# Three changes to a four-layer image kernel on one core: where group statistics are taken, which output sums are added first, and the instruction order of a spline attention

## The chip, the cores and the metric

The kernel runs on one core of one Trainium2 chip. The time is the device time of one launch in microseconds (us); lower is better. Everything is float32.

A core has TensorE (PE, matrix products; its weight loads are shown as PEld), VectorE (DVE), ScalarE (ACT) and GpSimd (POOL), each with an instruction queue of its own that is worked off in order; SyncE (SP) issues the transfers. The engines wait for one another by semaphores. SBUF is the on-chip memory with 128 partitions, PSUM the memory that PE writes its products to.

## The reference

`x` is (2, 256, 56, 56). Four layers are applied in turn, each to the group-normalised `x`, and each is added to `x`. `_gn` normalises over groups of 8 channels and all pixels of an image.

```python
x = x + _L0_conv_ref(_gn(x), ...)   # 7x7 neighbourhood attention, 8 heads, no softmax
x = x + _L1_conv_ref(_gn(x), ...)   # 4x4 depthwise blur
x = x + _L2_conv_ref(_gn(x), ...)   # channel gate, then softmax attention over all 3136 pixels
x = x + _L3_conv_ref(_gn(x), ...)   # attention whose scores pass a spline, 4 heads of 32
```

The last layer takes nearly all of the time:

```python
sim = jnp.einsum('bhnd,bhdm->bhnm', q, k) / math.sqrt(dh)      # 2 images, 4 heads, 3136 x 3136
xs = jnp.clip(sim, -6, 6)
kan = base_w * silu(xs) + jnp.einsum('...k,k->...', b_splines(xs), coef)   # cubic spline
attn = softmax(kan, axis=-1)
out = jnp.einsum('bhnm,bhmd->bhnd', attn, v)
```

Every score needs a clip, the silu, a cubic spline with knots 2.4 apart, and the exponential.

## The kernel before, in words

`x` stays in SBUF as `X`, 128 partitions by 4 units (image times channel half) by 3136 pixels. The layers follow one another: `opening`, `attention0` for image 0 and image 1, `group_norm_stats` "1", `blur1`, `group_norm_stats` "2", `attention2`, `group_norm_stats` "3", `attention3`. Every function is one or more blocks, and at a block's end all engines meet, so what one engine does there counts unless another of the same block ends later.

**Group statistics.** `group_norm_stats` (L373) issues 28 `bn_stats` on DVE, one for each unit and each chunk of 448 pixels (L400), aggregates them with four `bn_aggr` (L403), and a short chain over PE and ACT makes `m.rstd` and `m.nbias`. For "2" the 28 `bn_stats` were already issued inside `blur1` (L970).

**Output of layer 0.** `project_out0` (L850) goes through eight spans of columns for two channel halves f, 16 jobs in all. PE makes a sum in one of eight PSUM banks (L866), DVE adds it to `X` (L879). The five spans of 500 columns (50 by 10 inner pixels) come first, then three spans for the borders of the image: 314, 294 and 48 columns; the last is four small pieces of 9 or 12 elements for each half.

**Projections of layers 0 and 2.** In `project_queries0` (L452) DVE normalises one unit (L461) and is then idle while PE and ACT make the queries. In `project2` (L1063) DVE makes the gated input (L1087) and then adds a bias to seven chunks (L1091), while POOL adds the gated input to `X` of the same image (L1080) and ACT copies the other two projections.

**Spline attention.** `kan_attention3` (L1483) handles 196 blocks: 2 images by 2 pairs of heads by 49 tiles of 64 queries. The 128 partitions hold 64 queries of each of two heads. The 3136 keys of a block are four quarters g of 784 (two PSUM banks of 392, index j). For one quarter:

- PE `scores(g)` makes the raw scores into `scp` (L1617).
- DVE `clip(g, 0)` and `clip(g, 1)` write `x` (L1696), 392 elements each.
- ACT `tanh` writes S back into `scp` (L1779); `magnitude` makes `a = |x|` (L1787); `beyond` makes `v1 = relu(a - 1.2)` and `v2 = relu(a - 3.6)` (L1795); `squared` their squares `s1`, `s2` (L1804).
- POOL `line` and `square` make `inner`, the polynomial part (L1580, L1587); `cube(g, 0)` and `cube(g, 1)` turn the squares into cubes (L1594).
- PE `right_side(g)` makes `up`, the part of the spline that holds for positive x only, from the cubes and two diagonal matrices (L1630).
- DVE `gate(g)` writes `up` where x > 0 into `prob` (L1689), `add_tanh` starts `fp` (called a_kan in the trace, L1707), `times_x` multiplies (L1714), `left(g, 0)` and `left(g, 1)` add the cubes (L1725), `add_right` sums into `prob` and finds the maximum (L1735).
- `row_max` (L1750) and `negated_max` (L1755) make the softmax shift once a block; ACT `exponent` (L1831) applies it; PE `turn` transposes `prob` in seven chunks (L1642), ACT `copies` moves each to SBUF (L1812), PE `weigh` multiplies it with V (L1652). `invert` (L1746), `place` (L1820), `fold_heads` (L1670), `keep_o` (L1826), `project_out` (L1662) and `add_output` (L1742) finish a block.

The order of each engine's queue is written out by hand: a list of (stage, lag), walked by `pipeline_pairs` (L1330), where lag is how many blocks behind the newest one the stage works. One walk is four **slots** g = 0..3, one per quarter. On DVE slot g clips quarter g of the newest block and finishes the quarter three slots back (called g3), and its last instruction is the gate of the quarter two back:

```python
order += [(add_tanh(g3), l3)] + between[0] + [(times_x(g3), l3)] + between[1] + [(left(g3, 0), l3), (clip(g, 0), 0), (left(g3, 1), l3),
          (clip(g, 1), 0), (add_right(g3), l3), (gate(g2), l2)]
```

`between` holds the small ones: invert in slot 1 and row_max in slot 3 behind add_tanh, add_output in slot 2 and negated_max in slot 3 behind times_x. Three handshakes tie the slots together. `scores` of a slot waits for that slot's `add_tanh`, because S and the scores share PSUM; the slot's first clip waits for `scores`. `tanh` on ACT waits for the slot's last clip, and the next slot's `add_tanh` waits for `tanh`. `gate` waits for `right_side`, which waits for the cubes. `invert` (slot 1) waits for `weigh(6)`, which PE issues in slot 0.

Of the kernel before, what the change touches and what calls it, by code (L numbers as in the profile page):

```python
# [7 lines left out]
F32 = mybir.dt.float32  # L8
ALU = mybir.AluOpType
# [4 lines left out]
B = 2  # L14
# [122 lines left out]
def conv_preact_kernel(nc, x, qkv_w, qkv_b, proj_w, proj_b, rel_bias, fir, cfc, theta_w, theta_b,  # L137
                       phi_w, phi_b, g_w, g_b, out_w, out_b, wq3, wk3, wv3, wo3, base_w, spline_w,
                       spline_scaler, mask_dram, spline_m, out):
    with ExitStack() as ctx:  # L140
        def sb(name, shape):
            return ctx.enter_context(nc.sbuf_tensor(name, shape, F32))
# [21 lines left out]

        m.onehot = sb("onehot", [KEYS, ONEHOT_W])
        bias_dram = nc.dram_tensor("bias_rows_dram", (BIAS_ROWS, BIAS_ROW), F32, kind="Internal").ap()

        with ExitStack() as early:
# [5 lines left out]
            stats2 = early.enter_context(nc.sbuf_tensor("blur_stats", [P, UNITS, CHUNKS, 6], F32))  # L174
            blur1(nc, m, stats2)
            group_norm_stats(nc, m, "2", stats2)
        attention2(nc, m)
        group_norm_stats(nc, m, "3")
# [194 lines left out]
def group_norm_stats(nc, m, tag, counted=None):  # L373

    with ExitStack() as st:
        sem = st.enter_context(signals(nc, tag))
        sb = lambda name, shape: st.enter_context(nc.sbuf_tensor(name + tag, shape, F32))
        stats = counted if counted is not None else sb("stats", [P, UNITS, CHUNKS, 6])
# [9 lines left out]
        with nc.Block() as block:  # L388
            @block.vector
            def _(dve):  # L390
# [6 lines left out]
                if counted is None:  # L397
                    for u in range(UNITS):
                        for k in range(CHUNKS):
                            link(dve.bn_stats(stats[:, u, k, :], m.X[:, u, CHUNK * k:CHUNK * (k + 1)]))  # L400
                    dve.wait_ge(chain, done[0])
# [50 lines left out]
def project_queries0(nc, m, b, xn, Q, O, qb, scale):  # L452
    with ExitStack() as st:
        sem = st.enter_context(signals(nc, f"p0_{b}"))
        qp = [st.enter_context(nc.psum_tensor(f"qp{i}_{b}", [P, 8, IMG], F32)) for i in range(4)]
        normed, cleared, q_made, q_placed, qb_ready = (sem(n) for n in ("xn_ready", "cleared", "q_made", "q_placed", "qb_ready"))
        with nc.Block() as block:
            @block.vector
            def _(dve):
# [3 lines left out]
                dve.wait_ge(qb_ready, 1)  # L463

# [385 lines left out]
def project_out0(nc, m, b, O):  # L850

    with ExitStack() as st:
        sem = st.enter_context(signals(nc, f"p0_{b}"))
        yp = [st.enter_context(nc.psum_tensor(f"yp{i}_{b}", [P, 512], F32)) for i in range(8)]
        y_made, y_added = sem("y_made"), sem("y_added")
        slots = EXTRA + DX_STEP
        spans = [(500 * k, 500) for k in range(5)] + [(slots, 314), (PAIR0 + 6, 294), (CORNER0, 48)]
        with nc.Block() as block:
# [11 lines left out]
            def _(dve):  # L870
                for n in range(2 * len(spans)):
# [12 lines left out]
                    if k < 5:  # L884
                        add(img[:, 3 + 10 * k:13 + 10 * k, 3:53], grid(0, 10, GRID, GRID))
                    elif k == 5:
                        add(img[:, 0:3, 3:53], grid(0, 3, DX_STEP, GRID))
                        add(img[:, 53:56, 3:53], grid(3 * DX_STEP + BOTTOM_SHIFT, 3, DX_STEP, GRID))
                    elif k == 6:
# [7 lines left out]
                    last[0].then_inc(y_added, 1)  # L897
                dve.wait_ge(y_added, 2 * len(spans))
# [164 lines left out]
def project2(nc, m, b, theta, phi, gT, gate_scale, gate_bias):  # L1063

    with ExitStack() as st:
# [3 lines left out]
        gated, made, kept_a, kept_v, with_s = (sem(n) for n in ("gated", "made", "kept_a", "kept_v", "with_s"))  # L1069
# [3 lines left out]
        with nc.Block() as block:  # L1073
# [10 lines left out]
            def _(dve):  # L1084
# [3 lines left out]
                for k in range(CHUNKS):  # L1088
# [3 lines left out]
                                      m.gbias[low:P, :].unsqueeze(1).to_broadcast([P - low, tiles, P]), ALU.add).then_inc(kept_v, 1)  # L1092
                dve.wait_ge(kept_v, CHUNKS)
# [389 lines left out]
def kan_attention3(nc, m, k3, out):  # L1483
# [3 lines left out]
    with ExitStack() as st:  # L1487
# [10 lines left out]
        v1 = [sb(f"v1{g}", [P, QUART]) for g in range(2)]  # L1498
# [373 lines left out]
```

## Time and profile before

| what | value |
|---|---|
| median of 3 runs | 7107.38 us (7102.32 to 7118.62) |
| the profiled execution | 7109.38 us, span 7107.3 us |
| busy: PE, DVE, ACT, POOL | 6218.9, 6060.1, 5703.7, 5398.8 us |
| mean granted clock of TensorE | 0.969 of full speed |
| moved by DMA | 79.83 MB, mean 11 GB/s |

The busy shares in tenths, in 40 slices of the span (178 us each), show the layers: nine or ten slices for layers 0 to 2, then thirty of one unchanging pattern.

```profile
PE   6777899996888888888888888888888888888888
DVE  5444444444999999999999999999999999999998
ACT  5372332333999999999999999999999999999998
POOL 4351000003999999999999999999999999999997
```

In the trace an instruction's record runs from the start of its execution to the acknowledged write, and the record of the next may begin before that end. So what an instruction takes of its engine is read from one start to the next, not from its duration; this is called its **step** below.

### The profile page before, as it was taken

What the parts mean: (1) busy time and instruction counts of PE and PEld (TensorE: products, weight loads), DVE (VectorE), ACT (ScalarE), POOL (GpSimd) and SP (SyncE); (2) the same over time, 40 slices, a digit from 0 to 9 for tenths busy, and PEclk for the clock granted to TensorE, in tenths of its full rate; (3) what the DMA queues carried; (4) which work ended last, traced back from release to release, by engine and by line L of the source; (5) the groups of instructions that cost most, each with busy time, mean ns of one, the idle gap of its engine ahead of it and who ended that gap; (6) DMA issues with size and microseconds to landing.
All of it is one profiled execution on the core that took longest, in us unless ns stands there. A gap on an engine that the chain in (4) does not pass through costs nothing. (4 is left out here: it accounts for less than half of the span.)

```text
span 7107.3 us, 136255 instructions
## 1 busy us (share of the span) xinstructions
PE 6218.9 (88%) x38014; PEld 4169.0 (59%) x38014; DVE 6060.1 (85%) x9428; ACT 5703.7 (80%) x8984; POOL 5398.8 (76%) x3379
## 2 busy tenths in 40 slices
PE   6777899996888888888888888888888888888888
PEld 4545676763555555555555555555555555555555
DVE  5444444444999999999999999999999999999998
ACT  5372332333999999999999999999999999999998
POOL 4351000003999999999999999999999999999997
PEclk8786999997999999999999999999999999999999
DMA  3221000002000000000000000100000000000000
GB/s 98 67 69 44 1 0 0 0 0 65 11 1 1 1 1 1 1 11 1 1 1 1 1 1 2 29 1 1 1 1 1 1 2 1 4 4 4 4 4 6
DMA packets 110735, 79.83 MB, mean 11 GB/s; under 512 B 68490, under 2 KB 108290, under 8 KB 109826
## 3 DMA queue, kind: packets, MB, share of 16 engines
q1 hardware_dynamic: 107306, 77.71, 3.8%
q8 instruction: 77, 1.26, 0.1%
q10 hardware_dynamic: 3288, 0.33, 0.0%
q14 instruction: 64, 0.52, 0.0%
HBM read 48.70 MB, written 22.86 MB: 10 GB/s over the span
## 5 line engine op out<-in xcount | busy, mean ns | idle before, releaser
L1594 POOL TENSOR_TENSOR a_s<-a_s,a_v 128x784 f32<-128x784 f32 x1568 | 2910.7, 1856 | 310.0 <-ACT a_s L1804 298.1
L1630 PE MATMUL a_right_sides<-a_s,diag_d 128*128 128x392 f32 x6272 | 2288.9, 508 | 14.7 <-POOL a_s L1594 1.0
L1630 PEld LDWEIGHTS a_right_sides<-a_s,diag_d 128*128 128x128 f32 x6272 | 1134.3, 191 | 1064.7 <-POOL a_s L1594 345.3
L1725 DVE SCALAR_TENSOR_TENSOR a_kan<-a_s,spline_c,a_kan 128x784 f32<-128x784 f32 x1568 | 1622.2, 1035 | 51.4 <-DVE a_kan L1714 0.9
L1587 POOL TENSOR_TENSOR a_inner<-a_inner,a_x 128x784 f32<-128x784 f32 x784 | 1458.9, 1861 | 0.0
L1804 ACT ACTIVATE a_s<-a_v 128x784 f32<-128x784 f32 x1568 | 1335.2, 852 | 4.6
L1795 ACT ACTIVATE a_v<-a_a 128x784 f32<-128x784 f32 x1568 | 1335.1, 852 | 0.3
L1652 PEld LDWEIGHTS a_weighed<-a_V,a_probT 128*128 128x128 f32 x9800 | 1232.4, 192 | 162.2
L1652 PE MATMUL a_weighed<-a_V,a_probT 128*128 128x65 f32 x9800 | 1223.5, 269 | 0.0
L1642 PE MATMUL a_turned<-ident,a_prob 128*128 128x128 f32 x4900 | 794.0, 280 | 325.8 <-ACT a_probT L1812 323.7
L1617 PE MATMUL a_scores<-a_K,a_q 32*64 32x392 f32 x6272 | 703.8, 515 | 273.0 <-DVE a_kan L1707 241.8
L1696 DVE TENSOR_SCALAR a_x<-a_scores 128x392 f32<-128x392 f32 x1568 | 876.1, 559 | 19.2 <-PE a_scores L1617 19.2
L1779 ACT ACTIVATE a_scores<-a_x 128x784 f32<-128x784 f32 x784 | 649.0, 828 | 260.3 <-DVE a_x L1696 248.1
L1642 PEld LDWEIGHTS a_turned<-ident,a_prob 128*128 128x128 f32 x4900 | 560.2, 147 | 465.4 <-ACT a_probT L1812 350.4
L1714 DVE SCALAR_TENSOR_TENSOR a_kan<-a_kan,linear,a_x 128x784 f32<-128x784 f32 x784 | 817.8, 1043 | 14.1
L1707 DVE SCALAR_TENSOR_TENSOR a_kan<-a_scores,half_base,a_inner 128x784 f32<-128x784 f32 x784 | 811.7, 1035 | 0.0
L1580 POOL TENSOR_SCALAR a_inner<-a_x,spline_c 128x784 f32<-128x784 f32 x784 | 782.9, 999 | 0.0
L1812 ACT COPY a_probT<-a_turned 128x512 f32<-128x512 f32 (+2 forms) x1372 | 724.5, 528 | 56.9 <-PE a_turned L1642 39.9
L1689 DVE SCALAR_TENSOR_TENSOR a_prob<-a_x,a_right_sides 128x784 f32<-128x784 f32 x784 | 757.0, 966 | 13.5 <-PE a_right_sides L1630 13.5
L1735 DVE CUSTOM_DVE_ANT_0 a_prob<-a_kan,a_prob 128x784 f32<-128x784 f32 x784 | 756.8, 965 | 0.6 <-DVE a_kan L1725 0.6
L1831 ACT ACTIVATE a_prob<-a_prob,a_nmax 128x784 f32<-128x784 f32 x784 | 735.3, 938 | 0.0
L1787 ACT ACTIVATE a_a<-a_x 128x784 f32<-128x784 f32 x784 | 662.6, 845 | 19.3 <-DVE a_x L1696 17.0
(198 smaller groups left out, 5293.8 us busy)
## 6 DMA issues: line engine op xcount, KB each, us to landing
rows<-bias_rows_dram SPq DMA_DIRECT2D x112, 91.0 KB
ve<-v_dram SPq DMA_DIRECT2D x98, 104.0 KB
X<-in_x_dram SPq DMA_DIRECT2D x4, 1568.0 KB, 13.8
xn<-kt SPq DMA_DIRECT2D x56, 112.0 KB, 2.2
v_dram<-vt SPq DMA_DIRECT2D x56, 112.0 KB, 2.0
a_q<-q_dram SPq DMA_DIRECT2D x392, 16.0 KB, 2.0
mask<-in_window_mask_dram SPq DMA_DIRECT2D x56, 98.0 KB, 1.9
a_V<-v_dram SPq DMA_DIRECT2D x4, 812.5 KB, 8.6
```

What stands on the lines that cost most here:

```text
L1580: eng.tensor_scalar(inner[g % 2][:, :], x[g][:, :], c[:, 0:1], c[:, 1:2], ALU.mult, ALU.add).then_inc(line_made, 1)
L1587: eng.tensor_tensor(z, z, x[g][:, :], ALU.mult).then_inc(inner_made, 1)
L1594: eng.tensor_tensor(s, s, v, ALU.mult).then_inc(cubed, 1)
L1630: mm = eng.matmul(up[:, j, 0:SUB], steps[i][:, :], cubes[g][:, SUB * j:SUB * (j + 1)], start=(i == 0), stop=(i == 1))
L1642: mm = eng.transpose(tp[:, j, :], prob[r][:, at:at + P], m.ident[:, :])
L1652: mm = eng.matmul(op[:, :], probT[(r + ch) % 2][:, j, :], V[p % 2][:, k, :], start=(k == 0), stop=(k == KEY_TILES3 - 1))
L1696: eng.tensor_scalar(x[g][:, SUB * j:SUB * (j + 1)], scp[:, j, 0:SUB], 6.0, -6.0, ALU.min, ALU.max).then_inc(clipped, 1)
L1707: eng.scalar_tensor_tensor(F, S, half_base[:, :], banked(inner[g % 2][:, :]), ALU.mult, ALU.add).then_inc(with_tanh, 1)
L1714: eng.scalar_tensor_tensor(F, F, linear[:, :], banked(x[g][:, :]), ALU.add, ALU.mult).then_inc(based, 1)
L1725: eng.scalar_tensor_tensor(F, banked((s1, s2)[j][g][:, :]), c[:, 3 + j:4 + j], F, ALU.mult, ALU.add).then_inc(left_added, 1)
L1795: eng.activation((v1, v2)[j][g % 2][:, :], a[:, :], ACT.Relu, bias=(-KNOT_IN, -KNOT_OUT)[j]).then_inc(v_ready, 1)
L1804: eng.activation((s1, s2)[j][g][:, :], (v1, v2)[j][g % 2][:, :], ACT.Square).then_inc(s_ready, 1)
```

## The change

It does three things.

1. **Statistics inside projections.** One buffer `m.stats` holds all units' statistics. For "1", image 0's 14 `bn_stats` are issued in `project_queries0` of image 1, and image 1's 14 in its `project_out0`, as chunks of rows become final. For "3", image 0's 14 are issued in `project2` of image 1, two behind each chunk's bias add; image 1's 14 stay in `group_norm_stats`.
2. **Border sums first.** In `project_out0` the three border spans come ahead of the five inner ones.
3. **Spline attention.** On DVE the gate is cut into two halves of 392, now in the slot of its own quarter, one ahead of and one behind `add_tanh`; the second clip is cut into two pieces of 196; the clips stand between the instructions of the chain; the small ones stand behind the first gate half. `row_max` is dropped: `add_right` stores the negated values and their minimum, and `exponent` applies scale -1. On ACT the two squares become one instruction of 1568 elements, behind the late copy. On POOL the two cubes become one of 1568, behind line and square. On PE four of the seven `turn` go right behind a `scores`, `turn(6)` with one more block of lag.

```diff
-def group_norm_stats(nc, m, tag, counted=None):
+def group_norm_stats(nc, m, tag, units=()):
...
+                for u in units:
+                    for k in range(CHUNKS):
+                        link(dve.bn_stats(stats[:, u, k, :], m.X[:, u, CHUNK * k:CHUNK * (k + 1)]))
@@ project_queries0, vector
                 dve.wait_ge(qb_ready, 1)
+                if b:
+                    for v in range(HALVES * (b - 1), HALVES * b):
+                        for k in range(CHUNKS):
+                            dve.bn_stats(m.stats[:, v, k, :], m.X[:, v, CHUNK * k:CHUNK * (k + 1)]).then_inc(counted, 1)
+                    dve.wait_ge(counted, HALVES * CHUNKS)
@@ project_out0
-        spans = [(500 * k, 500) for k in range(5)] + [(slots, 314), (PAIR0 + 6, 294), (CORNER0, 48)]
+        spans = [(slots, 314), (PAIR0 + 6, 294), (CORNER0, 48)] + [(500 * k, 500) for k in range(5)]
...
+                    if b == B - 1 and f == 1 and k >= 3:
+                        dve.wait_ge(y_added, n + 1)
+                        whole = range((10 * k - 27) // 8, (10 * k - 17) // 8 if k < 7 else CHUNKS)
+                        for v in range(HALVES):
+                            for c in whole:
+                                dve.bn_stats(m.stats[:, HALVES * b + v, c, :], ...).then_inc(counted, 1)
@@ project2, vector, in the loop over chunks k
+                    if b:
+                        for v in range(HALVES * (b - 1), HALVES * b):
+                            dve.bn_stats(m.stats[:, v, k, :], m.X[:, v, CHUNK * k:CHUNK * (k + 1)]).then_inc(counted, 1)
@@ kan_attention3, gpsimd
-                    order += [(line(g2), l2), (cube(g2, 1), l2), (square(g2), l2), (cube(g1, 0), l1)]
+                    order += [(line(g2), l2), (square(g2), l2), (cubes(g1), l1)]
@@ kan_attention3, tensor
-                pipeline_pairs(pe, [(scores(0), 0), (right_side(2), 1), (weigh(5), 3), (weigh(6), 3), (turn(0), 2),
-                                      (scores(1), 0), (project_out, 4), (right_side(3), 1), (turn(1), 2), (weigh(0), 2), (turn(2), 2),
-                                      (fold_heads, 3), (scores(2), 0), (right_side(0), 0), (weigh(1), 2), (turn(3), 2), (weigh(2), 2), (turn(4), 2),
-                                      (scores(3), 0), (right_side(1), 0), (weigh(3), 2), (turn(5), 2), (weigh(4), 2), (turn(6), 2)])
+                pipeline_pairs(pe, [(scores(0), 0), (turn(6), 3), (right_side(2), 1), (weigh(5), 3), (weigh(6), 3), (turn(0), 2),
+                                      (scores(1), 0), (project_out, 4), (right_side(3), 1), (turn(1), 2), (weigh(0), 2),
+                                      (fold_heads, 3), (scores(2), 0), (turn(2), 2), (right_side(0), 0), (weigh(1), 2), (turn(3), 2), (weigh(2), 2),
+                                      (scores(3), 0), (turn(4), 2), (right_side(1), 0), (weigh(3), 2), (turn(5), 2), (weigh(4), 2)])
@@ kan_attention3, vector
-                        eng.scalar_tensor_tensor(banked(part(r, g)), banked(x[g][:, :]), 0.0, U, ALU.is_gt, ALU.mult).then_inc(right_gated, 1)
+                        eng.scalar_tensor_tensor(part(r, g)[:, at], x[g][:, at], 0.0, up[:, j, 0:SUB], ALU.is_gt, ALU.mult).then_inc(right_gated, 1)
...
+                        first, end = ((0, SUB), (SUB, SUB + SUB // 2), (SUB + SUB // 2, 2 * SUB))[j]
...
-                        eng.tensor_tensor_reduce(out=f, in0=F, in1=f, scale=1.0, scalar=-3.0e38, op0=ALU.add, op1=ALU.max,
+                        eng.tensor_tensor_reduce(out=f, in0=F, in1=f, scale=-1.0, scalar=3.0e38, op0=ALU.add, op1=ALU.min,
...
+                    eng.tensor_reduce(nmax[r][:, :], gmin[r][:, :], AX.X, ALU.min).then_inc(max_ready, 1)
...
+                    g3, l3 = (g - 3) % 4, int(g < 3)
+                    small = {1: [(invert, 3)], 2: [(add_output, 4)], 3: [(negated_max, 1)]}.get(g, [])
+                    order += [(gate(g3, 0), l3)] + small + [(add_tanh(g3), l3), (gate(g3, 1), l3), (times_x(g3), l3), (clip(g, 0), 0), (left(g3, 0), l3),
+                              (clip(g, 1), 0), (left(g3, 1), l3), (clip(g, 2), 0), (add_right(g3), l3)]
@@ kan_attention3, scalar
-                    order += [(tanh((g - 2) % 4), int(g < 2))] + [(keep_o, 3)] * (g == 2) + [(magnitude(g), 0), early, (beyond(g, 0), 0), e, (beyond(g, 1), 0),
-                              (squared(g, 0), 0), late, (squared(g, 1), 0)]
+                    order += [(tanh((g - 2) % 4), int(g < 2))] + [(keep_o, 3)] * (g == 2) + [(magnitude(g), 0), early, (beyond(g, 0), 0), e, (beyond(g, 1), 0), late, (squared(g), 0)]
```

## Rows read from the trace of the kernel before

**Rows 1.** Busy us (instructions) of PE, PEld, DVE, ACT, POOL; clock, DMA share, GB/s.

```profile
2000.00:7000.00 5000.00, 4454.09 (x26519) 2921.66 (x26518) 4935.92 (x7316) 4713.85 (x6950) 4729.07 (x2927) 1.00 0.01 3
```

**Rows 2.** Who waited for whom, 2000 to 7000 us: total, times, longest.

```profile
PE a_scores L1617 <- DVE a_kan L1707: 214.3, 267, 1.2
DVE a_prob L1689 <- PE a_right_sides L1630: 4.0, 2, 2.8
```

**Rows 3.** Timeline of DVE, slot 1 of one block: start, duration, instruction.

```profile
4008.63 0.96 DVE L1689 SCALAR_TENSOR_TENSOR a_prob<-a_x,a_right_sides 128x784 f32<-128x784 f32 x1
4009.52 1.03 DVE L1707 SCALAR_TENSOR_TENSOR a_kan<-a_scores,half_base,a_inner 128x784 f32<-128x784 f32 x1
4010.46 0.16 DVE L1746 RECIPROCAL a_rinv<-a_weighed 128x1 f32<-128x1 f32 x1
4010.59 1.04 DVE L1714 SCALAR_TENSOR_TENSOR a_kan<-a_kan,linear,a_x 128x784 f32<-128x784 f32 x1
4011.74 1.04 DVE L1725 SCALAR_TENSOR_TENSOR a_kan<-a_s,spline_c,a_kan 128x784 f32<-128x784 f32 x1
4012.68 0.56 DVE L1696 TENSOR_SCALAR a_x<-a_scores 128x392 f32<-128x392 f32 x1
4013.16 1.03 DVE L1725 SCALAR_TENSOR_TENSOR a_kan<-a_s,spline_c,a_kan 128x784 f32<-128x784 f32 x1
4014.10 0.56 DVE L1696 TENSOR_SCALAR a_x<-a_scores 128x392 f32<-128x392 f32 x1
4014.57 0.96 DVE L1735 CUSTOM_DVE_ANT_0 a_prob<-a_kan,a_prob 128x784 f32<-128x784 f32 x1
4015.46 0.96 DVE L1689 SCALAR_TENSOR_TENSOR a_prob<-a_x,a_right_sides 128x784 f32<-128x784 f32 x1
```

**Rows 4.** The same timeline, slot 2 around add_output, and slot 1 of the next block.

```profile
4016.35 1.03 DVE L1707 SCALAR_TENSOR_TENSOR a_kan<-a_scores,half_base,a_inner 128x784 f32<-128x784 f32 x1
...
4018.37 0.28 DVE L1742 TENSOR_TENSOR X<-X,a_right_sides 128x128 f32 x1
4018.56 1.04 DVE L1725 SCALAR_TENSOR_TENSOR a_kan<-a_s,spline_c,a_kan 128x784 f32<-128x784 f32 x1
...
4035.95 0.96 DVE L1689 SCALAR_TENSOR_TENSOR a_prob<-a_x,a_right_sides 128x784 f32<-128x784 f32 x1
```

**Rows 5.** Timeline of DVE in project_out0, five small border pieces merged into one line.

```profile
657.23 0.76 DVE L879 SCALAR_TENSOR_TENSOR X<-yp,pbias,X 128x12 f32<-128x12 f32 x5
```

**Rows 6.** Timelines of PE, and of DVE's add_tanh, slot 0; PE's scores of slot 2.

```profile
4002.69 1.03 DVE L1707 SCALAR_TENSOR_TENSOR a_kan<-a_scores,half_base,a_inner 128x784 f32<-128x784 f32 x1
4003.78 0.89 PE L1617 MATMUL a_scores<-a_K,a_q 32*64 32x392 f32 x8
4007.33 1.67 PE L1652 MATMUL a_weighed<-a_V,a_probT 128*128 128x65 f32 x14
4008.84 0.61 PE L1642 MATMUL a_turned<-ident,a_prob 128*128 128x128 f32 x4
4017.80 0.89 PE L1617 MATMUL a_scores<-a_K,a_q 32*64 32x392 f32 x8
```

**Rows 7.** Timelines of ACT (a tanh) and of POOL (a cube of 784).

```profile
4014.69 0.83 ACT L1779 ACTIVATE a_scores<-a_x 128x784 f32<-128x784 f32 x1
4002.72 1.85 POOL L1594 TENSOR_TENSOR a_s<-a_s,a_v 128x784 f32<-128x784 f32 x1
```

**Rows 8.** Timeline of DVE: a sum of project_out0, then group_norm_stats "1"; brackets: idle before.

```profile
652.69 0.74 DVE L879 SCALAR_TENSOR_TENSOR X<-yp,pbias,X 128x500 f32<-128x500 f32 x1 [0.94 <-PE yp L866]
...
659.27 14.85 DVE L400 BATCH_NORM_STATS2 stats<-X 128x6 f32<-128x448 f32 x28 [0.88 <-PEq L128]
```

**Rows 9.** Timelines: DVE in project2, DVE and ACT in project_queries0, each of image 1.

```profile
1196.90 0.69 DVE L1091 TENSOR_TENSOR gT<-pp,gbias 128x512 f32<-128x512 f32 x1 [4.10 <-PE pp L1123]
358.35 0.15 DVE L462 TENSOR_SCALAR qb<-qkvb 128x2 f32<-128x2 f32 x1
381.05 2.90 ACT L497 ACTIVATE Q<-qp,qb 128x250 f32<-128x250 f32 x12 [0.56 <-PE qp L480]
```

More of the change, by code:

```diff
@@ L395, in link @@
                     ins.then_inc(chain, 1)
[L397 to L400, printed above, removed]
+                for u in units:
+                    for k in range(CHUNKS):
+                        link(dve.bn_stats(stats[:, u, k, :], m.X[:, u, CHUNK * k:CHUNK * (k + 1)]))
+                if units:
                     dve.wait_ge(chain, done[0])
@@ L1623, in stage @@
                         n = 4 * t + g
-                        eng.wait_ge(right_gated, n + 1)
+                        eng.wait_ge(right_gated, 2 * n + 2)
                         if g == 0:
                             eng.wait_ge(x_added, t + 1)
-                        for i, cubes in enumerate((s1, s2)):
-                            eng.wait_ge(cubed, 2 * n + i + 5)
+                        eng.wait_ge(cubed, n + 3)
+                        for i in range(2):
                             for j in range(2):
-                                mm = eng.matmul(up[:, j, 0:SUB], steps[i][:, :], cubes[g][:, SUB * j:SUB * (j + 1)], start=(i == 0), stop=(i == 1))
+                                mm = eng.matmul(up[:, j, 0:SUB], steps[i][:, :], s[g][:, i, SUB * j:SUB * (j + 1)], start=(i == 0), stop=(i == 1))
                         mm.then_inc(right_made, 1)
@@ L1764, in _ @@
                 for g in range(4):
-                    (g2, l2), (g3, l3) = (((g - back) % 4, int(g < back)) for back in (2, 3))
-                    between = {1: ([(invert, 3)], []), 2: ([], [(add_output, 4)]), 3: ([(row_max, 1)], [(negated_max, 1)])}.get(g, ([], []))
-                    order += [(add_tanh(g3), l3)] + between[0] + [(times_x(g3), l3)] + between[1] + [(left(g3, 0), l3), (clip(g, 0), 0), (left(g3, 1), l3),
-                              (clip(g, 1), 0), (add_right(g3), l3), (gate(g2), l2)]
+                    g3, l3 = (g - 3) % 4, int(g < 3)
+                    small = {1: [(invert, 3)], 2: [(add_output, 4)], 3: [(negated_max, 1)]}.get(g, [])
+                    order += [(gate(g3, 0), l3)] + small + [(add_tanh(g3), l3), (gate(g3, 1), l3), (times_x(g3), l3), (clip(g, 0), 0), (left(g3, 0), l3),
+                              (clip(g, 1), 0), (left(g3, 1), l3), (clip(g, 2), 0), (add_right(g3), l3)]
                 pipeline_pairs(dve, order)
@@ L1830, in stage @@
                         eng.wait_ge(max_ready, t + 1)
-                        eng.activation(part(r, g), part(r, g), ACT.Exp, bias=nmax[r][:, :]).then_inc(exp_done, 1)
+                        eng.activation(part(r, g), part(r, g), ACT.Exp, scale=-1.0, bias=nmax[r][:, :]).then_inc(exp_done, 1)
                     return stage
```

90 lines of the change are left out of this document (46 added, 44 removed).

## The prediction

> **What bounds the kernel now.** I read the 40 slices first: thirty of them are the spline attention, so a change there counts 196 times. Then the busy times inside it: DVE is busy 4936 of 5000 us, POOL 4729, ACT 4714, PE 4454 [rows 1]. Then the waits: in those 5000 us PE waited 214 us for DVE's add_tanh, while DVE waited 4.0 us for any other engine, in two places [rows 2]. DVE sets the pace. Last, its timeline, read by steps: the slot runs from gate to gate, 4008.63 to 4015.46, 6.83 us [rows 3], and the block 27.32 us, four equal slots [rows 3, 4].
>
> A saturated DVE can still lose time between its own instructions, and the busy time hides it, since records overlap. The steps show it. add_tanh, which writes PSUM, has the step 0.94 when something independent follows (the reciprocal, 4010.46); so have both `left`. But times_x, which needs add_tanh's result, starts 1.07 behind it, and the first left 1.15 behind times_x [rows 3]. So 0.13 and about 0.20 us are spent waiting for a result of DVE itself: **0.33 a slot**. The small instructions sit in these gaps free of charge: from add_tanh to the first left it is 2.22 us with a reciprocal between [rows 3] and 2.21 with add_output [rows 4].
>
> **The attention on DVE, per block.** The new order puts an independent instruction behind each link of the chain: the second gate half (step 0.48) behind add_tanh, a clip of 392 behind times_x, a clip piece of 196 behind each left.
> - The gaps go: 4 x 0.33 = 1.32 us saved. Behind the lefts a clip of 0.48 is replaced by one of 0.27: 0.94 + 0.27 = 1.21 from left to dependent, where a left lasts 1.04 and the wait behind times_x adds 0.11 (4011.63 to 4011.74 [rows 3]). 0.06 us of cover is left, so no new gap; without that cover it would be a few hundredths.
> - Two cuts a slot. A clip of 392 has the step 0.475, a gate of 784 has 0.89; both read PSUM and write SBUF [rows 3]. Twice 0.475 is 0.95, so a cut costs 0.06; by the slope the 196 piece has 0.475 - 0.21 = 0.27, again about 0.06 more for the cut. I take 0.065: 8 x 0.065 = 0.52 added. The other end is the tiniest piece: five of 12 elements span 0.76 us, with the last one's tail about 0.14 each [rows 5], nearly all fixed. 196 and 392 lie nearer to the rows of 392 and 784, so I take 0.065 and keep 0.14 for a rival.
> - The small ones lose their cover. invert and negated_max at the reciprocal's step 0.13, add_output 0.19 (4018.37 to 4018.56) [rows 3, 4]: 0.45 added; row_max, which cost nothing, goes. These steps may be stretched by the gap they stood in: the lower end is the cut's 0.065 for each of the two, some 0.12 less a block.
> - The maximum of add_right becomes a minimum, exp gets a scale: same operands and sizes, costed at nothing.
>
> Sum: 0.52 + 0.45 - 1.32 = **-0.35 us a block**.
>
> **What is late next.** DVE's slot is now about 6.63 us.
> - *scores.* From add_tanh's start to the slot's first clip there were 0.94 + 0.13 + 1.15 + 0.94 = 3.16 us, now 0.94 + 0.48 + 0.94 = 2.36. In slot 0 scores end 1.98 behind add_tanh's start (4004.67), in slot 2, behind fold_heads, 2.34 (4018.69) [rows 4, 6]. It fits, with 0.38 and 0.02 to spare; slot 2 should also start earlier than before, since a turn ahead of fold_heads has moved away. If PE were late, the clips and everything behind them on DVE would be late with it.
> - *tanh.* From the last clip's end to the next add_tanh: (0.27 - 0.35) + 0.89 + 0.48 = 1.29; tanh needs 0.03 + 0.83 [rows 3, 7]. 0.43 to spare.
> - *invert.* weigh(6) ended 6.31 behind slot 0's add_tanh (4009.00 against 4002.69) [rows 6]. turn(6) now stands ahead of it: three tiles, three quarters of the four tiles' 0.61 less an overlap of 0.16 (weigh: 1.67 long, step 1.51), 0.34 [rows 6]. So weigh(6) ends at 6.65, and invert, ahead of add_tanh on DVE, could go at 6.63. With a few hundredths for the signal I cost this at **0.05 a block**; add_tanh, and so scores, wait with it.
> - *cubes.* One instruction of 1568, at most 2 x 1.85 = 3.7 us [rows 7], where right_side could start on the first half before. POOL's work was 4729 / 5000 of a slot, 6.46 us [rows 1], and one wide instruction doesn't add to it: under 6.63. right_side was done where weigh starts, 4.64 behind slot 0's add_tanh; with turn(6) ahead it is 4.98, and the gate is due at 6.63 - 0.48 = 6.15 [rows 6], so late cubes have 1.2 us before DVE sees them. ACT saves one instruction's fixed part per slot, nothing on the path. No transfer and no queue of SP is changed.
>
> So -0.30 a block, x 196 = **-59 us**. The pipelines' filling and draining I leave as they are.
>
> **The statistics.** A `bn_stats` of 448 has the step 14.85 / 28 = 0.53 [rows 8].
> - "1": all 28 leave group_norm_stats, -14.85. Image 0's 14 (7.4 us) start at about 358.5 in project_queries0 and end near 366, under ACT, which works to 384 [rows 9]; free. Image 1's: in project_out0 two 500-column jobs come each 3.36 us (0.74 + 0.94, twice) with 1.5 of DVE work [rows 8]; two statistics fit, four (2.1) overrun by 0.3, which eight banks absorb. But the last four follow the last sum: +2.1 and 0.1 of wait. Net -12.6.
> - Border sums first: same jobs, same PE time; zero. It is what lets the statistics be spread at all.
> - "3": 14 leave, -7.4. In project2 a pair (1.06) fits into the 4.1 us that DVE waits each chunk [rows 9]; the last pair comes behind the last bias add, +1.1. Net -6.3.
> - A few more semaphores to clear at block ends: hundredths each.
>
> Sum -59 - 19 = -78. The profiled execution took 7109.4 us (span 7107.3), which gives 7031; the median of the runs lies 2 us lower, so **7030 us**.
>
> **The rivals.**
> - *Waits for another engine take the place of DVE's gaps* (0.20). For it: scores in slot 2 has 0.02 us to spare, invert none, all engines are over 90% busy but PE (89%). Against it: PE, ACT and POOL have idle time in the block now, and it stands just where the new order wants it (PE waits for add_tanh). Half the block's gain lost is 7060; all of it 7090.
> - *Short instructions cost more: slower* (0.10). If each cut costs 0.14 as the tiny pieces do [rows 5], a block gets 8 x 0.14 + 0.45 - 1.32 = +0.25, +49 us, and with the statistics 7109 + 49 - 19, less 2: 7137. All in all the change breaks even at 0.117 a cut: (1.32 - 0.45 + 19 / 196) / 8, without the wait of invert. Against it: 392 elements take 0.475, which leaves 0.06. The Trainium skill has a rule here (Perfetto Trace Analysis, Optimizing Scalar/DVE Operations): a fixed cost of about 60 ns on SBUF and 125 ns on PSUM, and larger instructions where the engine is saturated; an estimate by its 125 for clip and gate, which read PSUM, would be +0.13 a block and about 7113. In this trace it is the PSUM writers that pay more (0.94 for 784), the readers 0.89.
> - *The gaps are not waits* (0.02). Were the 0.13 and 0.20 part of the instructions, cuts and small ones would be pure cost: 0.97 x 196 = 190, 7278. The small instructions that fit in at no cost [rows 3, 4] speak against it. The Trainium skill (VectorE: DVE Perf Modes, The DRAIN you can't avoid) says that a semaphore between chained instructions costs nothing; by that rule this is what would happen, and the steps here, 1.07 against 0.94, disagree.
>
> **How the numbers follow.** The forecast's case has 0.68; it alone spans 7006 (small ones cheap, -24) to 7045 (invert and scores a little worse). The range 7005 to 7090 takes in the lateness rival and leaves out the last two, 0.12. A measurement here can tell 0.2%, 14 us, from no change. Faster: 0.68 and three quarters of the lateness rival, 0.83. Same: the rest of it and a milder form of the short-instruction rival, 0.07. Slower: 0.10.
>
> **What would show it.** Right: a DVE slot of 6.6 to 6.7 us; step 0.94 from add_tanh to the gate half and 0.94 from times_x to the clip; clip pieces at 0.27; reciprocal 0.13 behind the gate half; no DVE waits for PE scores. Wrong: 196 pieces at 0.34 or more; DVE idle ahead of the first clip for scores, ahead of the reciprocal for weigh, or ahead of add_tanh for tanh. group_norm_stats "1" without statistics, "3" with 14; projections 2 and 1 us longer.

## The result, and the profile after

| kernel | median | lowest to highest | ratio to before, 95% interval |
|---|---|---|---|
| before | 7105.17 us (4 runs) | 7102.32 to 7118.62 | |
| changed | 7068.47 us (4 runs) | 7064.50 to 7086.07 | 0.9949 [0.9928, 0.9971] |

37 us faster, where 78 were forecast; the time lies inside the range and on the side given. The profiled execution is the slowest of the four, 7086.07 us, span 7084.3.

The answer to [rows 1], with the same columns:

```profile
2000.00:7000.00 5000.00, 4397.14 (x26546) 2948.20 (x26545) 4951.64 (x8606) 4667.57 (x6225) 4657.47 (x2199) 0.99 0.01 3
```

DVE is still the busiest. One figure is new: TensorE's mean clock, 1.00 before, is 0.99. The answer to [rows 2], who waited for whom from 2000 to 7000 us:

```profile
PE a_scores L1632 <- DVE a_kan L1727: 372.3, 507, 1.2
PE a_scores L1685 <- DVE a_kan L1727: 230.5, 183, 1.3
DVE a_prob L1705 <- PE a_right_sides L1645: 42.8, 42, 1.0
```

PE now waits 603 us for add_tanh instead of 214: with fold_heads (L1685) there is a wait of 1.26 us in each block (230.5 us over 183 waits). And DVE, which waited for PE twice, waits 42 times, about 1.0 us each, in its gate (L1705).

An undisturbed slot on DVE's timeline (start, duration), to be read beside [rows 3]:

```profile
4003.99 0.56 DVE L1705 SCALAR_TENSOR_TENSOR a_prob<-a_x,a_right_sides 128x392 f32<-128x392 f32 x1
4004.47 1.03 DVE L1727 SCALAR_TENSOR_TENSOR a_kan<-a_scores,half_base,a_inner 128x784 f32<-128x784 f32 x1
4005.41 0.55 DVE L1705 SCALAR_TENSOR_TENSOR a_prob<-a_x,a_right_sides 128x392 f32<-128x392 f32 x1
4005.89 1.03 DVE L1734 SCALAR_TENSOR_TENSOR a_kan<-a_kan,linear,a_x 128x784 f32<-128x784 f32 x1
4006.83 0.56 DVE L1714 TENSOR_SCALAR a_x<-a_scores 128x392 f32<-128x392 f32 x1
4007.30 1.03 DVE L1745 SCALAR_TENSOR_TENSOR a_kan<-a_s,spline_c,a_kan 128x784 f32<-128x784 f32 x1
4008.24 0.36 DVE L1714 TENSOR_SCALAR a_x<-a_scores 128x196 f32<-128x196 f32 x1
4008.51 1.03 DVE L1745 SCALAR_TENSOR_TENSOR a_kan<-a_s,spline_c,a_kan 128x784 f32<-128x784 f32 x1
4009.45 0.36 DVE L1714 TENSOR_SCALAR a_x<-a_scores 128x196 f32<-128x196 f32 x1
4009.74 0.97 DVE L1755 CUSTOM_DVE_ANT_0 a_prob<-a_kan,a_prob 128x784 f32<-128x784 f32 x1
...
4010.64 0.56 DVE L1705 SCALAR_TENSOR_TENSOR a_prob<-a_x,a_right_sides 128x392 f32<-128x392 f32 x1
...
4011.16 0.17 DVE L1766 RECIPROCAL a_rinv<-a_weighed 128x1 f32<-128x1 f32 x1
4011.35 1.04 DVE L1727 SCALAR_TENSOR_TENSOR a_kan<-a_scores,half_base,a_inner 128x784 f32<-128x784 f32 x1
```

The slot takes 6.65 us (4003.99 to 4010.64), and the gaps are gone: 0.94 from add_tanh to the gate half, 0.94 from times_x to the clip, 0.94 from each left to its clip piece. From one reciprocal to the next, the median over the attention is 27.04 us, against 27.32 before.

So where are the other 41 us? On PE's timeline, around one of the 42 waits (brackets: idle before, and who ended it), and below it DVE's gate of the same slot:

```profile
4100.40 0.33 PE L1685 MATMUL a_scores<-fold_heads,a_by_query 128*64 128x64 f32 x2 [1.26 <-DVE a_kan L1727]
4100.66 0.89 PE L1632 MATMUL a_scores<-a_K,a_q 32*64 32x392 f32 x8
4101.48 0.87 PE L1657 MATMUL a_turned<-ident,a_prob 128*128 128x128 f32 x4
4102.14 4.31 PE L1645 MATMUL a_right_sides<-a_s,diag_d 128*128 128x392 f32 x8
...
4106.60 0.56 DVE L1705 SCALAR_TENSOR_TENSOR a_prob<-a_x,a_right_sides 128x392 f32<-128x392 f32 x1 [1.04 <-PE a_right_sides L1645]
```

and the windows of 2 us there (PE, PEld, DVE, ACT, POOL busy; TensorE's clock ahead of the last two figures):

```profile
4100.00:4102.00 2.00, 1.60 (x14) 0.92 (x15) 2.00 (x4) 2.00 (x4) 2.00 (x2) 0.94 0.00 0
4102.00:4104.00 2.00, 2.00 (x5) 1.16 (x4) 2.00 (x4) 1.93 (x3) 1.92 (x2) 0.50 0.00 0
4104.00:4106.00 2.00, 2.00 (x6) 1.09 (x5) 1.56 (x4) 1.73 (x4) 1.79 (x2) 0.70 0.00 0
```

PE stands still for 1.26 us, and 1.4 us after it has started again the granted clock falls to half, 1.2 GHz, for 3.4 us. The eight matmuls of right_side take 4.31 us there; at the full clock, three blocks earlier, it was 2.80:

```profile
4020.86 2.80 PE L1645 MATMUL a_right_sides<-a_s,diag_d 128*128 128x392 f32 x8
```

The gate on DVE comes 1.04 us late, and the block is 1.2 us longer (1.15 to 1.27). From 1800 to 7000 us the clock's record has 43 such stretches; before it had two. In all 43 PE had stood still ahead of fold_heads and had started again 0.4 to 1.4 us before. But it does so in every block, 191 times in all, and most of these stops bring no fall. Mean block over the steady attention (186 blocks): 27.30 us against 27.03 undisturbed; 196 x 0.27 is 53 us.

### The profile page after: what moved, and what is told of

It reads as the page before. It is cut to its first block and busy times, and to the rows that moved or that the text cites. A ratio compares the mean times of both kernels' runs of the same rounds, so it can differ in the third digit from the quotient of the medians.

```text
span 7084.3 us, 132922 instructions
## 1 busy us (share of the span) xinstructions
PE 6159.0 (87%) x38014; PEld 4202.7 (59%) x38014; DVE 6069.4 (86%) x10800; ACT 5648.1 (80%) x8200; POOL 5317.2 (75%) x2595
## 3 DMA queue, kind: packets, MB, share of 16 engines
q8 instruction: 77, 1.26, 0.1%
## 5 line engine op out<-in xcount | busy, mean ns | idle before, releaser
L1609 POOL TENSOR_TENSOR a_s<-a_s,a_v 128x1568 f32<-128x1568 f32 x784 | 2766.4, 3529 | 321.3 <-ACT a_s L1820 299.9
L1645 PEld LDWEIGHTS a_right_sides<-a_s,diag_d 128*128 128x128 f32 x6272 | 1167.3, 196 | 722.0 <-issue 71.7
L1820 ACT ACTIVATE a_s<-a_v 128x1568 f32<-128x1568 f32 x784 | 1186.4, 1513 | 5.0
L1714 DVE TENSOR_SCALAR a_x<-a_scores 128x196 f32<-128x196 f32 (+1 forms) x2352 | 995.1, 423 | 20.3 <-PE a_scores L1632 20.3
L1705 DVE SCALAR_TENSOR_TENSOR a_prob<-a_x,a_right_sides 128x392 f32<-128x392 f32 x1568 | 869.6, 555 | 55.8 <-PE a_right_sides L1645 55.8
L1657 PE MATMUL a_turned<-ident,a_prob 128*128 128x128 f32 x4900 | 813.6, 285 | 2.2 <-ACT a_probT L1828 1.2
```

Source lines behind the costliest of these rows:

```text
L1609: eng.tensor_tensor(both, both, v[g % 2][:, :, :].rearrange("p j c -> p (j c)"), ALU.mult).then_inc(cubed, 1)
L1645: mm = eng.matmul(up[:, j, 0:SUB], steps[i][:, :], s[g][:, i, SUB * j:SUB * (j + 1)], start=(i == 0), stop=(i == 1))
L1657: mm = eng.transpose(tp[:, j, :], prob[r][:, at:at + P], m.ident[:, :])
L1705: eng.scalar_tensor_tensor(part(r, g)[:, at], x[g][:, at], 0.0, up[:, j, 0:SUB], ALU.is_gt, ALU.mult).then_inc(right_gated, 1)
L1714: ins = eng.tensor_scalar(x[g][:, first:end], scp[:, bank, first - SUB * bank:end - SUB * bank], 6.0, -6.0, ALU.min, ALU.max)
L1820: eng.activation(s[g][:, :, :].rearrange("p j c -> p (j c)"), v[g % 2][:, :, :].rearrange("p j c -> p (j c)"), ACT.Square).then_inc(s_read ...
```

## Experiments

The theory: the new order on DVE gives what was worked out, and TensorE's clock, let down by a wait that the new order on PE made longer, takes part of it back. In the table are the readings of each kernel's own profile; a "low stretch" is one at 1.2 GHz between 1800 and 7000 us (the only one of e2, at 6988 us, and the only one of e6, at 6991 us, lie where the pipeline already drains), "block" is the median from one reciprocal to the next, and "waits" are PE's stops in slots 0 to 3 of one undisturbed block near 4000 us.

```
kernel                    time us  ratio to before [95%]     low   block   PE's waits in a block
before                    7105.2                               2   27.32   0.59 1.16 0.77 0.33
changed                   7068.5   0.9949 [0.9928, 0.9971]    43   27.04   1.08 0.89 1.26 0.22
e1_old_pe                 7112.7   1.0014 [1.0005, 1.0023]     0   27.46   0.71 0.89 0.96 0.74
e2_twice_turn1            7027.7   0.9897 [0.9882, 0.9912]     1   27.03   1.08 0.80 0.83 0.22
e3_stats_only             7099.4   0.9996 [0.9987, 1.0005]     2   27.32
e4_attention_only         7086.2   0.9978 [0.9968, 0.9988]    35   27.07
e5_twice_turn5            7070.5   0.9932 [0.9919, 0.9946]    37   27.04   0.64 0.89 1.26 0.21
e6_half_turn1             7027.1   0.9874 [0.9859, 0.9889]     1   27.03   1.07 0.80 1.04 0.21
e7_stats_twice_turn1      7103.3   0.9980 [0.9971, 0.9989]     3   27.32
e8_no_piece_behind        7163.3   1.0065 [1.0052, 1.0079]     0   27.72   1.28 0.96 1.03 0.42
e9_stats_filled_end       7085.3   0.9965 [0.9951, 0.9978]     1   27.31
e10_half_filled_end       7022.2   0.9877 [0.9862, 0.9893]     0   27.03
e11_gate_whole            7143.0   1.0046 [1.0032, 1.0060]     0   27.62   1.18 0.86 1.15 0.58
```

The kernel before, run again beside them, had medians of 7103.8 us (e1 to e4), 7116.0 (e5 to e8) and 7113.0 (e9 to e11), and single runs from 7096 to 7129. So kernels of different groups are compared by their ratios, and through their profiles.

**PE's list as before (e1), and turn(1) issued twice (e2).**

```diff
 e1: the stage list of pipeline_pairs(pe, ...) is that of the kernel before
 e2, in turn(ch):
-                        for j, k in enumerate(turned3(ch)):
+                        for _ in range(2 if ch == 1 else 1):
+                            for j, k in enumerate(turned3(ch)):
```

> The changed kernel with TensorE's list of stages as it was before (turn(2) ahead of fold_heads again, turn(6) in slot 3). Theory A, the clock: in the changed kernel's trace TensorE is at 1.2 GHz in 45 short stretches of the attention, each right behind the 1.26 us in which it waits ahead of fold_heads, and each makes that block 1.2 us longer, some 52 us in all. With turn(2) back in that wait, the stretches should be 5 or fewer; turn(2) has to wait for the copy of chunk 1, so fold_heads and the scores of slot 2 come 0.1 to 0.2 us late for the clip, 20 to 40 us. Expected 7030 to 7055. Theory B, lateness: it is not the clock, and TensorE's new list is what keeps the engines from waiting; with the old one VectorE waits more than in the changed kernel. Expected 7070 to 7100.

> The changed kernel, with the four transposes of turn(1) issued twice (the same result in the same place), which is 0.44 us more of TensorE work per block in the idle time ahead of fold_heads, and nothing else. Theory A, the clock: TensorE waits 0.8 instead of 1.26 us there, the stretches at 1.2 GHz go (5 or fewer), every block takes 27.0 us, and the kernel is faster for doing more work: 7015 to 7030. Theory B, lateness: more work on TensorE gives nothing back: 7068 to 7090.

e1: no low stretch is left, and yet it is slower than the kernel before. DVE's timeline shows why (times_x, then the slot's first clip):

```profile
4006.27 1.03 DVE L1734 SCALAR_TENSOR_TENSOR a_kan<-a_kan,linear,a_x 128x784 f32<-128x784 f32 x1
4007.45 0.57 DVE L1714 TENSOR_SCALAR a_x<-a_scores 128x392 f32<-128x392 f32 x1
```

The step is 1.18 us where it should be 0.94, in two or three of a block's four slots (once 1.28): the clip waits for `scores`. On PE, what stands ahead:

```profile
4005.65 0.66 PE L1657 MATMUL a_turned<-ident,a_prob 128*128 128x128 f32 x4 [0.97 <-ACT a_probT L1828]
```

In the old list two turns follow each other closely ahead of scores, and the second waits 0.97 us for ACT to copy the first. The old order on DVE left scores 3.16 us, the new one 2.36. So the new list on PE is needed by the new order on DVE. This run does not separate the two theories by its time, since it takes away one loss and brings another; both expectations were missed.

e2 adds nothing useful, only 0.44 us of repeated work in front of the long wait. It runs 41 us faster than the changed kernel, at 7027.7 us. The block stays at 27.03, one low stretch is left, and the waits for fold_heads are shorter, 0.9 us at the longest:

```profile
PE a_scores L1686 <- DVE a_kan L1728: 151.7, 185, 0.9
```

**The same work in another place (e5), and half of it (e6).**

```diff
 e5: as e2, with ch == 5
 e6, ahead of the loop in turn(ch):
+                        if ch == 1:
+                            for j in range(2):
+                                at = first_key3(turned3(ch)[j])
+                                eng.transpose(tp[:, j, :], prob[r][:, at:at + P], m.ident[:, :])
```

> The changed kernel with the four transposes of turn(5) issued twice: the same 0.44 us of repeated TensorE work a block as with turn(1) doubled, but in slot 3, behind scores(3), and not ahead of fold_heads. (P) the place matters: TensorE's wait ahead of fold_heads in slot 2 stays about 1.26 us, its clock goes on falling to 1.2 GHz in 30 to 45 short stretches, and the time stays at 7060 to 7095. (S) only the amount of TensorE work in a block matters: the low stretches go (0 to 5 are left) and the time is 7020 to 7035, as with turn(1) doubled.

> The changed kernel with two of the four transposes of turn(1) issued twice: half the dose, about 0.22 us of repeated work ahead of fold_heads. If the clock goes by how long TensorE stands still there, its wait is about 1.05 us and the low stretches are fewer than the 43 of the changed kernel and more than the 1 of the full dose: between 7028 and 7068, 7045 as the middle. If what doubling does comes by another way (the spacing of weigh and turn, say), I would not expect a result between the two: 7068 or 7028.

e5 is (P), the place: PE is busy for 4474 us of the 5000, more than in e2 (4450), and the clock falls 37 times all the same. The stop ahead of fold_heads is as long as it was:

```profile
4019.26 0.33 PE L1686 MATMUL a_scores<-fold_heads,a_by_query 128*64 128x64 f32 x2 [1.26 <-DVE a_kan L1728]
```

e6 missed the range that it gave for the length of the stop: half the dose already gives everything, 7027.1 us with one low stretch. That is one of the two values it gave for the case that doubling works by something else than the length. The wait there is 1.04 us:

```profile
4024.37 0.33 PE L1689 MATMUL a_scores<-fold_heads,a_by_query 128*64 128x64 f32 x2 [1.04 <-DVE a_kan L1731]
```

So the loss does not grow with the wait ahead of fold_heads; it is there at 1.26 us and gone at 1.04. The sum of the waits does not order the kernels (3.45 us a block in the changed one, 3.00 in e5, both with falls; 3.12 in e6, without). Nor does the longest single wait. The kernel before, and e8 further down, stand still ahead of scores like this:

```profile
4010.61 0.89 PE L1617 MATMUL a_scores<-a_K,a_q 32*64 32x392 f32 x8 [1.16 <-DVE a_kan L1707]
```

```profile
4018.30 0.89 PE L1632 MATMUL a_scores<-a_K,a_q 32*64 32x392 f32 x8 [1.28 <-DVE a_kan L1727]
```

The kernel before has some 100 such stops of 1.16 us, and its two falls come 0.3 and 1.6 us after two of them. e8 stands still for 1.2 us or more 183 times, mostly 1.28, longer than the changed kernel ahead of fold_heads, and its clock does not fall once. It is not a matter of PE being busier either: e8 (4332 us of the 5000) and e11 (4310) have PE busy least of all, and neither has a fall. So what is shown is that filling this one stop takes the falls away and that the same work elsewhere does not. The length of a stop alone does not decide; what runs around it counts too, and what of it was not separated.

**The two halves of the change alone (e3, e4), and the end of the kernel (e7, e9).**

```diff
 e3: kan_attention3 as before, all else as changed
 e4: kan_attention3 as changed, all else as before
 e7: e3 with turn(1) issued twice, as in e2
 e9, e3 with, in turn(ch):
+                        for _ in range(5 if isinstance(t, int) and t == BLOCKS3 - 2 and ch == 2 else 1):
```

> The statistics inside projections and the border sums first, with the spline attention as it was before. By the prediction's sum 19 us faster than before; in the trace of the changed kernel all that lies ahead of the attention's first finished block is some 25 us earlier, some of which may be the attention's own start. Expected 7080 to 7087 where the kernel before takes 7105, TensorE at 1.2 GHz in at most 5 stretches of the attention.

> The new spline attention alone, with the statistics and the border sums as before. If the parts add: the changed kernel's time plus 19 to 25 us, 7085 to 7095, and some 40 stretches at 1.2 GHz under theory A. If the stretches depend on how the blocks happen to lie against the chip's own beat, their number may differ, at 1.2 us each.

> The old attention with the new statistics and border order (it measured 7099, where 7085 was expected), and in it the four transposes of turn(1) issued twice. In that kernel the attention began 21 us earlier and 14 of it were gone by the last reciprocal, in the last 75 us, where TensorE's clock is at 1.2 GHz for longer than before. (C) the low clock in the drain takes it: more work on TensorE keeps the clock up longer there, the last 75 us are some 10 us shorter and the time is 7085 to 7092. (O) it has nothing to do with TensorE: 7099, or a few us more for the repeated work in the drain. The steady blocks should stay at 27.32 us in either case, since the clock was full there already.

> The old attention with the new statistics and border order once more, and in it, once in the whole run, the transposes of turn(2) of the last but one block issued five times: 1.76 us of repeated work where TensorE stood still for 2.03 us ahead of a fold_heads, right before its clock stayed low to the end (in the run with turn(1) doubled throughout that wait was still 1.59 us, and the clock fell all the same). (C) that wait took the clock down and the low clock took the statistics' gain: the last two steps between reciprocals shrink from 17.4 and 18.1 us to about 14 and 11, and the time is 7085 to 7090. (O) the clock goes low there for another reason, since the work grows thin in the drain anyway: 7099.

e4 has the changed kernel's loss, 35 low stretches, and its 7086.2 us lie in the range given. e3 was a surprise: its attention starts 21 us earlier than before (first reciprocal at 1776.7 us against 1797.8), and the time is the same within the interval. From first to last reciprocal the attention takes 5315.4 us where it took 5301.7. Its blocks are 27.32 as before; the last three steps between reciprocals are 29.7, 17.4 and 18.1 us, and were 27.2, 13.7 and 11.1. Windows of 20 us, first of the kernel before, then of e3:

```profile
7080.00:7100.00 20.00, 17.98 (x150) 16.61 (x149) 6.31 (x13) 12.45 (x25) 0.00 (x0) 1.00 0.00 1
```

```profile
7060.00:7080.00 20.00, 17.47 (x93) 16.15 (x92) 7.86 (x15) 9.22 (x17) 0.00 (x0) 0.62 0.00 0
7080.00:7100.00 20.00, 14.59 (x67) 13.70 (x66) 0.74 (x3) 4.36 (x10) 0.00 (x0) 0.50 0.07 24
```

While the pipeline drains, DVE has little left and PE is the busy engine: its clock is the end's clock. In e3 it fell behind this wait, and stayed down to the end:

```profile
7063.22 0.30 PE L1688 MATMUL a_scores<-fold_heads,a_by_query 128*64 128x64 f32 x2 [2.03 <-DVE a_kan L1725]
...
7070.85 3.09 PE L1670 MATMUL a_weighed<-a_V,a_probT 128*128 128x65 f32 x14
```

The fourteen matmuls of weigh take 1.67 us in the kernel before [rows 6]. e7 did not get there: 7103.3 us, by ratio a little better than e3 (0.9980 against 0.9996, the intervals overlap), but its attention is no shorter (5316.8 us from first to last reciprocal); that wait was still 1.59 us, and the clock was low from 7065.6 on. By itself this result would have spoken for (O). e9 fills the same wait with repeated transposes, once in the run:

```profile
7054.87 2.37 PE L1661 MATMUL a_turned<-ident,a_prob 128*128 128x128 f32 x20
7057.53 0.30 PE L1689 MATMUL a_scores<-fold_heads,a_by_query 128*64 128x64 f32 x2 [0.29 <-DVE a_kan L1726]
...
7073.99 1.67 PE L1671 MATMUL a_weighed<-a_V,a_probT 128*128 128x65 f32 x14
```

The clock stays up until 4 us before the end, the last two steps are 13.7 and 11.1 us again, and the time is 7085.3 us, ratio 0.9965 where e3 had 0.9996: (C), within the range given. So the statistics and the border order do bring 20 to 25 us (21 by e3's first reciprocal, 25 by e9's ratio), and in e3 the clock of the last 40 us had swallowed most of it.

**The gaps and cuts on DVE (e8, e11).**

```diff
 e8, e2 with, in clip and in the order of DVE:
-                        first, end = ((0, SUB), (SUB, SUB + SUB // 2), (SUB + SUB // 2, 2 * SUB))[j]
+                        first, end = ((0, SUB), (SUB, 2 * SUB))[j]
-                              (clip(g, 1), 0), (left(g3, 1), l3), (clip(g, 2), 0), (add_right(g3), l3)]
+                              (clip(g, 1), 0), (left(g3, 1), l3), (add_right(g3), l3)]
 e11, e6 with the gate in one piece of 784 ahead of the small ones:
-                              (add_tanh(g3), l3), (gate(g3, 1), l3), (times_x(g3), l3)
+                              (add_tanh(g3), l3), (times_x(g3), l3)
```

> The changed kernel with turn(1) doubled (7027.7, clock full), and in it the clip of the second half left whole behind the first left, and nothing behind the second left, so that add_right follows its producer directly. One cut a slot is saved (0.27 + 0.27 - 0.475 = 0.065 us). (G) a result of DVE itself read by the next instruction costs about 0.20 us (0.13 at the least): a slot 0.065 to 0.135 longer, 784 slots: 7079 to 7133, the step from the second left to add_right 1.07 to 1.15 us, and a clip of 392 at 0.475. (N) the gaps are no waits: 784 x 0.065 = 51 us less, 6977.

> The changed kernel with half of turn(1) doubled (7027.1, clock full), and in it the gate in one piece of 784 ahead of the small instructions and add_tanh, so that times_x follows add_tanh directly in all four slots. (G) a cut saved, 2 x 0.475 - 0.89 = 0.06 us, and a gap paid, 1.07 - 0.94 = 0.13: +0.07 a slot, block 27.31, 7082; if this link costs as much as the one from the second left to add_right did (0.28), +0.22 a slot and 7200. (N) no gap: 784 x 0.06 = 47 less, 6980.

e8 is (G) and beyond its range. The last left, then add_right:

```profile
4000.65 1.03 DVE L1745 SCALAR_TENSOR_TENSOR a_kan<-a_s,spline_c,a_kan 128x784 f32<-128x784 f32 x1
4001.87 0.97 DVE L1755 CUSTOM_DVE_ANT_0 a_prob<-a_kan,a_prob 128x784 f32<-128x784 f32 x1 [0.20 <-DVE a_kan L1745]
```

The step is 1.22 us, 0.28 more than the engine needs, and it was 1.23 with the clip piece in between (4008.51 to 4009.74 in the slot above). So a piece of 196 there costs nothing at all: the gap has the same length with it and without. A slot is 0.20 us longer for the clip of 392 in the other place (0.48 against 0.27), the block 0.69: four times 0.20, less some 0.1 in the slot of the reciprocal, which no longer waits for weigh.

e11, at 7143.0 us, lies between the two values of (G). add_tanh and times_x stand 1.07 us apart in all four slots,

```profile
4002.91 1.03 DVE L1730 SCALAR_TENSOR_TENSOR a_kan<-a_scores,half_base,a_inner 128x784 f32<-128x784 f32 x1
4003.98 1.04 DVE L1737 SCALAR_TENSOR_TENSOR a_kan<-a_kan,linear,a_x 128x784 f32<-128x784 f32 x1
```

which is the 0.13 of [rows 3]. With the cut saved that makes 0.07 a slot as expected, 0.28 of the block's 0.59 us. The rest was not in the expectation: times_x to the clip is 0.97 or 0.98 instead of 0.94 (0.03 to 0.04 a slot), and in the slot of fold_heads it is 1.23, another 0.26, since the clip waits for scores (0.19 of it shows as idle time) now that the gate half no longer stands between add_tanh and it. Against that, the reciprocal's slot saves 0.1, as in e8.

**Both waits filled (e10).**

```diff
 e10, e6 with, in turn(ch):
+                        for _ in range(3 if isinstance(t, int) and t == BLOCKS3 - 2 and ch < 2 else 1):
```

> The changed kernel with half of turn(1) doubled (7027.1), and in it turn(0) and turn(1) of the last but one block issued three times, where TensorE stood still for 1.35 us ahead of project_out, right before its clock fell for 6.8 us. (C) with the wait cut to some 0.5 us the clock stays up there, the 5.6 us of that right_side become 2.9, the step between reciprocals there goes from 17.9 to about 14, and the time is 7022 to 7025. (O) the repeated work only delays what follows: 7027 to 7030.

As (C) has it, the clock stays up there, and the median, 7022.2 us, lies in its range, though the step between reciprocals came down only from 17.9 to 15.4 us. The row where the clock fell in e6, and the same one in e10:

```profile
6991.91 5.59 PE L1645 MATMUL a_right_sides<-a_s,diag_d 128*128 128x392 f32 x8
```

```profile
6986.16 2.90 PE L1645 MATMUL a_right_sides<-a_s,diag_d 128*128 128x392 f32 x8
```

That this makes the kernel faster is not shown: by ratio e6 and e10 cannot be told apart (0.9874 and 0.9877), and of the 5 us between the medians 3 are between the groups' kernels before. By the profiles the end is 2.4 us shorter (169.4 us against 171.8 from the reciprocal seven blocks before the last).

## Why the prediction was right and wrong

**The attention on DVE: right.** The gaps went as worked out. By term: a gate cut costs 0.48 + 0.47 - 0.89 = 0.06 us, a clip piece 0.27, the negated maximum only 0.06 to 0.07 (0.13 was the price), add_output 0.20. In the slot shown the reciprocal came 0.52 us behind the gate half and held add_tanh another 0.19 (4011.16 to 4011.35), 0.24 in all; the median over the attention is 0.52 and 0.11, 0.16 in all, against 0.13 + 0.05. In e8 and e11, where it waits for nothing, it is 0.08. ("Reciprocal 0.13 behind the gate half", among the signs of being right, was a slip: the gate half alone takes 0.48.) Add_right behind the last piece takes 1.23 us from the left instead of 1.21: the direct link measured in e8 is 1.22, so the 0.06 of cover was not there. What was 0.35 less a wait of 0.05 is, by the undisturbed blocks, 27.32 - 27.03 = 0.29. From the first reciprocal to the last, e2 needs 5243.9 us and the kernel before 5301.7: 58 us less, and -59 was forecast. The small ones came some 0.07 us a block cheaper than their price and the four steps to add_right some 0.08 dearer, so the closeness of the sum is in part luck.

**What is late next: right for what it looked at.** scores, tanh and cubes made DVE wait nowhere in an undisturbed block. e1 shows how little room scores had: with PE's old list the same slots miss by 0.24 us and more.

**The failed step** is one that the prediction did not take: it costed PE's list only by when its products come, and took the clock of 1.00 [rows 1] for granted. "PE, ACT and POOL have idle time in the block now, and it stands just where the new order wants it" was its argument against lateness, and "slot 2 should also start earlier than before, since a turn ahead of fold_heads has moved away" was noted as a gain. That very move let PE stand still for 1.26 us ahead of fold_heads in each block; with PE's old list (e1) that stop and the falls are gone. With the clock kept up by 0.22 us of repeated work, the kernel runs at 7027.1; forecast 7030 (by the ratios, taken of 7107, e6 would be at 7018 and e2 at 7034). The missing term is 43 falls x 1.2 us = 52 us in the profiled run, which is the slowest of the four. In the medians it is 41 us (7068.5 against 7027.7 and 7027.1). Why the clock falls behind some of these stops and not behind others, and behind none of e8's, stays open.

**"The pipelines' filling and draining I leave as they are": wrong.** From the reciprocal seven blocks before the last, the end took 169.0 us in the profile before, 183.2 in e3, 179.0 in the changed kernel, 170.6 in e2 and 171.8 in e9. The last 30 to 40 us are PE's, and its clock moves them by up to 14 us. The profiled execution adds up with it: the falls cost some 50 us, the end 10, the attention began 25 us earlier where 19 were forecast, and the span is 23 us shorter instead of 78.

**The statistics: right in size, as far as can be told.** The first aggregation of "1" starts at 674.1 and 666.1 us in the two profiles with the old statistics, and at 653.4 to 659.0 in the eleven with the new ones; the forecast of -12.6 lies within that. From there to the one of "3", which also holds the change in project2, it was 933.0 and 931.8 us, and is 926.3 to 929.6: 2 to 7 less, forecast -6.3. Which of the steps fell short cannot be read from profiles that scatter this much.

**The rivals.** Lateness (0.20, 7060 to 7090) came nearest to the number: DVE did wait for PE, and half the block's gain was lost. But it did not come where it was looked for, from scores or weigh; undisturbed blocks have no such wait. Short instructions (7137) is refuted by 0.06 for a cut. "The gaps are no waits" (7278) is refuted by e8 and e11: a direct link costs 0.13 us behind add_tanh and 0.28 ahead of add_right. The Trainium skill has its rule (VectorE: DVE Perf Modes, The DRAIN you can't avoid), that a semaphore between chained instructions costs nothing more, from a chain of copies with and without one. Here an instruction that waits for the result of the one ahead starts that much later than one that does not; a chain without the semaphore was not run. The break-even of a cut was added up wrong: (1.32 - 0.45 + 19 / 196) / 8 is 0.121, not 0.117, which changes nothing else.

## What to carry to other kernels

When an order is changed around a saturated engine, look at what each other engine does in the time it gains: a longer stop of TensorE is not free just because nobody waits for its product at that moment. Read the granted clock's record over the whole stage, with what PE did ahead of each fall, and not its mean (0.99 here hid 40 us); the longest wait need not be the one (e8), and before calling a part of a change useless, look at the clock of the last microseconds too: e3 measured nothing and had gained 20.

## What the runs showed of the hardware

- TensorE stood still for 1.26 us a block ahead of fold_heads and was busy for 88% of the time, and its clock fell to 1.2 GHz, mostly every fourth or fifth block (109 or 136 us apart); with the same stop cut to 1.04 us it fell once in 5200 us, at their end. The Trainium skill tells of such a trap (TensorE: Matmul & The Clock Gate, HAM oscillation) for a loop that stands still for DMA for several microseconds at a time; in this trace the stops are far shorter, and they end on VectorE.
- The length of the stop does not decide alone: e8 stood still for 1.28 us a block ahead of scores, with TensorE busy for 87% of the time, and its clock did not fall in 5200 us.
- A stretch of 3.4 us at the low clock costs this kernel 1.2 us: right_side alone is 1.5 us longer (4.31 against 2.80), and DVE's gate waits 1.04 of it.
- On DVE an instruction of 196 elements between a PSUM writer and the custom add_right that reads its result was entirely free: 1.23 us from the one to the other with it, 1.22 without.
